# Row tiles of sixteen rows of all eight batches, in an attention-and-experts kernel on one core

## What is computed

```python
v = layernorm(x)
kv = v[:, :, :, None, :] * ctx[:, :, None, :, :]      # every pair of 8 rows in a head: (8, 32, 8, 8, 512)
y = causal_convolution(kv, k) + kv * skip             # along the 512 columns, one filter for each head
x = x + einsum('bhijl,bhil->bhjl', y, ctx)            # mix: sum over the first row index
h = layernorm(x)                                      # 2048 tokens of 512
scores = sigmoid(h @ gate_w.T); two of 8 experts for a token, weights normalized, times 2.5
x = x + shared_ffn(h) + sum over the two experts of weight * expert_ffn(h)
```

## Time and profile before

| | |
|---|---|
| time, median of 3 runs | 721.83 us (719.22 to 723.05) |
| profiled execution: its own time | 725.05 us |
| its span in the trace | 723.3 us |
| PE busy | 658.7 us, 91% |
| DVE busy | 446.4 us, 62% |
| POOL busy | 351.5 us, 49% |
| ACT busy | 309.5 us, 43% |
| TensorE clock granted, mean | 0.975 of full |
| DMA moved | 91.6 MB, 127 GB/s |

### The profile page before, as it was taken

One profiled execution on the slowest core, in us unless ns is written; L12 is line 12 of the kernel. 1 busy time (PEld: TensorE's weight loads), 2 busy tenths in 40 slices (PEclk: granted clock), 3 DMA queues, 4 the chain that ended last, 5 costly groups with the idle time before them and its releaser, 6 DMA issues.

```text
span 723.3 us, 11575 instructions
## 1 busy us (share of the span) xinstructions
PE 658.7 (91%) x3475; PEld 330.7 (46%) x3476; DVE 446.4 (62%) x689; ACT 309.5 (43%) x422; POOL 351.5 (49%) x304
## 2 busy tenths in 40 slices
PE   5989878989979989989999998798879999999993
PEld 3535334444334444443444443345445555555551
DVE  5998894899897677797887767874331221122110
ACT  5386667373306464224631295534332233323321
POOL 2999897947468524578564016200222222322232
PEclk8999988999999999999999999999999999999998
DMA  7944224321145600134214659859995788898854
GB/s 203 288 121 127 60 87 88 73 58 45 55 151 123 154 15 16 30 132 79 69 29 176 274 122 350 276 117 193 223 179 98 128 127 128 134 133 131 132 81 58
DMA packets 130520, 91.58 MB, mean 127 GB/s; under 512 B 96992, under 2 KB 110816, under 8 KB 129952
## 3 DMA queue, kind: packets, MB, share of 16 engines
q1 hardware_dynamic: 121728, 71.49, 41.0%
q0 software_dynamic: 8176, 18.75, 14.5%
q10 hardware_dynamic: 576, 0.82, 0.5%
HBM read 46.32 MB, written 25.65 MB: 100 GB/s over the span
## 4 chain that ended last, share of the span: by engine, by line
PE 46%; DVE 16%; POOL 15%; DMA 8%; ACT 7%; issue 5%; SPq 1%; POOLq 1%; DVEq 0%; ACTq 0%
PE banks L844 14%; PE banks L845 14%; PE banks L846 13%; POOL arena L665 9%; DMA out<-xf,ids 5%; POOL arena L693 4%; DVE arena L1509 2%; PE banks L936 2%; POOL arena L732 1%; ACT arena L1264 1%; DMA mixT<-x_tok 1%; PE banks L940 1%; PE banks L941 1%; DVE hm L1655 1%; DVE stats L1522 1%
## 5 line engine op out<-in xcount | busy, mean ns | idle before, releaser
L665 POOL TENSOR_TENSOR arena<-arena 128x512 f32<-128x512 f32 x120 | 140.0, 1197 | 66.6 <-DVE arena L1495 37.1
L807 POOL DMA_INDIRECT out<-xf,ids x39 | 60.5, 1552 | 194.4 <-DMA out<-xf,ids 138.2
L844 PE MATMUL banks<-arena 128*128 128x512 f16 (+1 forms) x330 | 124.9, 379 | 19.8 <-DVE arena L1509 9.4
L845 PE MATMUL banks<-arena 128*128 128x512 f16 (+1 forms) x330 | 124.8, 378 | 0.0
L846 PE MATMUL banks<-arena 128*128 128x512 f16 (+1 forms) x330 | 124.8, 378 | 0.0
L844 PE MATMUL banks<-arena,normed 128*128 x312 | 98.5, 316 | 4.3 <-issue 4.3
L845 PE MATMUL banks<-arena,normed 128*128 x312 | 98.4, 315 | 0.0
L846 PE MATMUL banks<-arena,normed 128*128 x312 | 98.4, 315 | 0.0
L1147 ACT ACTIVATE arena<-arena 128x2048 f16<-128x2048 f32 x31 | 59.1, 1905 | 91.7 <-POOL arena L665 88.9
L1873 DVE SCALAR_TENSOR_TENSOR hm<-banks,silu 128x256 f32<-128x256 f32 x39 | 16.5, 424 | 123.8 <-PE banks L846 112.8
L1509 DVE TENSOR_TENSOR arena<-banks,arena 128x512 f32<-128x512 f32 x128 | 80.3, 681 | 11.3 <-PE banks L846 11.1
(11 more groups left out here) (205 smaller groups left out, 1093.5 us busy)
## 6 DMA issues: line engine op xcount, KB each, us to landing
arena<-split_filters SPq DMA_DIRECT2D x31, 256.0 KB
arena<-in_expert_w SPq DMA_DIRECT2D x12, 544.0 KB, 7.6
stages<-in_expert_w SPq DMA_DIRECT2D x10, 544.0 KB
arena<-in_ctx_hidden SPq DMA_DIRECT2D x4, 1024.0 KB, 7.8
arena<-in_ctx SPq DMA_DIRECT2D x8, 512.0 KB, 6.5
out<-x_tok SPq DMA_DIRECT2D x6, 512.0 KB, 5.6
x_tok<-in_expert_w SPq DMA_DIRECT2D x5, 544.0 KB, 5.5
mixT<-in_expert_w SPq DMA_DIRECT2D x5, 544.0 KB
```

The source lines that it names most:

```text
L665: nc.gpsimd.tensor_tensor(kv[s % 2][:, lb * COLS:(lb + 1) * COLS].rearrange("p (b j i) -> p b j i", i=NH, j=NH), v[:, a, None, :].to_broad ...
L807: nc.gpsimd.indirect_dma_start(out=out, out_offset=bass.IndirectOffsetOnAxis(ap=ids[slot][:, 0:1], axis=0), in_=yg[slot], in_offset=None, ...
L844: nc.tensor.matmul(dst, wh, xh, start=(k == 0), stop=False)
L845: nc.tensor.matmul(dst, wh, xl, start=False, stop=False)
```

## The change

- A row tile holds sixteen rows of all eight batches (RT = 16), which are two whole heads. `x_rows`, `ctx_rows`, `out_rows`, `skip_col` and `mixT` follow; loads and stores are four DMAs of one tile in place of two of 64 partitions.
- A step needs one tile of values (`outer` waits for tile h // 2), and a tile of results is whole after two steps. mix_out and mixed_tile of tiles 0, 1 and 2 move into their own group; the order of the two turn banks is rewritten for it.
- The beginning loads tile 0 first, turns it twice (bank 4 for DVE, bank 5 for ACT) and works the first step by block of the sequence. Tiles 2 and 3 are normalized later, behind the first steps. The filter's low half goes to POOL.
- The low half of step 10 goes from POOL to DVE. row_bases (five small DVE instructions in group 1) works out the token numbers on the chip. The second half of the pair work is earlier in group 2 (whole `pairs(1)` at h = 6), and send_rows(1) and (2) end their own group.
- In the last group three tiles are normalized early, the logits stand before down(3), and the order of expert pieces is changed. In the routed loop the four id loads stand behind the first hidden tile, and the loads and splits of experts 6 and 7 are one tile earlier.

The diff, cut to its core:

```diff
-DVE_LOWS = (0, 1, 3, 5, 6, 7, 8, 9) + tuple(range(2 * HG - 2, H, 2))
+DVE_LOWS = (0, 1, 3, 5, 6, 7, 8, 9, 10) + tuple(range(2 * HG - 2, H, 2))
-    x_rows = x.rearrange("b (g r) l -> g b r l", r=RG)
+    x_rows = x.rearrange("b (g q r) l -> g q b r l", q=Q, r=RT)
+        turn_order = turns("skip", 0) + turns("prep", 1) + turns("out", 0, range(0, Q - 1))
         for g in range(1, G):
+            turn_order += turns("out", g - 1, (Q - 1,)) + turns("feed", g - 1) + [("xf", g - 1, 0)]
...
+            turn_order += turns("skip", 1) if g == 1 else []
+            turn_order += turns("prep", g + 1, range(0, 2)) + turns("out", g, (0,)) + turns("prep", g + 1, range(2, Q))
+            turn_order += [("rank", g - 1, 0)] + turns("skip", g + 1, range(0, 2)) + turns("out", g, (1, 2))
+            turn_order += turns("skip", g + 1, range(2, Q))
...
+            first_inverse_root(0)
+            filter_low()
             first_inverse_root(1)
+            outer(1)
+            outer(2)
+            first_inverse_root(2)
+            low_parts(2)
+            first_inverse_root(3)
+            outer(3)
...
+            first_prepare(0)
+            first_convolve(0)
+            first_convolve(1)
+            first_prepare(1)
+            first_convolve(2)
+            first_convolve(3)
+            convolve(1)
+            first_prepare(2)
+            first_prepare(3)
...
+            prepare(1, range(2, Q))
+            mix_out(0, 0)
+            convolve(6)
+            mix_out(0, 1)
+            convolve(7)
+            mix_out(0, 2)
             for g in range(1, G):
                 convolve(s0)
-                mix_out(g - 1, range(0, 2))
                 down(g - 2, 0)
-                mix_out(g - 1, range(2, Q))
+                mix_out(g - 1, Q - 1)
...
                 gate_up(g - 1, 3)
+                mix_out(g, 0)
                 if g < G - 1:
                     prepare(g + 1, range(2, Q))
                     ranks(g - 1)
+                    convolve(s0 + 6)
+                    skip_sum(g + 1, 0)
+                    skip_sum(g + 1, 1)
+                    gate_up(g - 1, SM - 2)
+                    mix_out(g, 1)
+                    convolve(s0 + 7)
+                    mix_out(g, 2)
+                    skip_sum(g + 1, 2)
+                    skip_sum(g + 1, 3)
+                    gate_up(g - 1, SM - 1)
...
             first_outer(3)
             first_low(2)
             first_low(3)
+            dve.wait_ge(filt_stored, 16)
+            products(0, 0, 0, range(0, 2))
+            first_moments(2)
+            low_parts(1)
+            products(0, 0, 0, range(2, LB))
+            first_moments(3)
+            total(0, 0)
+            first_shift_by(2)
+            first_shift_by(3)
             skip_product(0, 0)
             skip_product(0, 1)
+            products(1, 1, 0)
+            total(1, 1)
             skip_term(0, 0)
             skip_product(0, 2)
             skip_term(0, 1)
             skip_product(0, 3)
...
                 for h in range(4, HG):
                     low_parts(s0 + h + 1)
-                    if g == G - 1 and h == 4:
+                    if g == G - 1 and h == 4 or g == 2 and h == 6:
                         pairs(g - 1)
-                    elif g < G - 1 and h == 6:
+                    elif g == 1 and h == 6:
                         pair_ranks(g - 1)
-                    elif g < G - 1 and h == 7:
+                    elif g == 1 and h == 7:
                         pair_rows(g - 1)
+                    products(s0 + h, h, g)
+                    if g < G - 1 and h == 7 or g == G - 1 and h == 6:
+                        mixed_tile(g, 2)
+                        mixed_stats(g, 2)
+                    total(s0 + h, h)
+                    if h == 5:
+                        mixed_tile(g, 0)
...
-        pieces_behind = {1: [(6, 0), (6, 1)], 3: [(6, 2)], 4: [(6, 3)]} | {c + 5: [(7, c)] for c in range(EX_PARTS)}
+        pieces_behind = {1: [(6, 0), (6, 1)], 2: [(6, 2)], 3: [(6, 3)]} | {c + 4: [(7, c)] for c in range(EX_PARTS)}
```

536 lines of the change are left out of this document (267 added, 269 removed).

## The result

The changed kernel takes 758.25 us (median of four runs, 757.26 to 758.67) where the kernel before takes 721.97 (719.22 to 723.05): a ratio of 1.0507, 95% interval 1.0476 to 1.0538. It is 36 us slower, outside the range of the prediction. The profiled executions took 758.67 us (span 756.8) against 725.05 (723.3), 33.6 more.

The account below looks back on a forecast made before the run. PE, busy 91% of the span, was taken as the bound. Terms -1.6 + 4.9 + 5.0 - 1.9 - 2.5 - 4.1 = -0.2 gave 721.6 us on the runs' scale, leaned to 720.5; range 707 to 731.

Parts of the forecast that it names:

- The opening: From the start to the first logits: step 3 late by 5.9 us, gains behind it, sum -1.6, bounds -8 and +5.
- Its chain: Opening: POOL's queued root of tile 3 delays DVE's skip products, ACT's value moments and turn_filter(3); step 3 5.9 us late.
- The give-back: Up to the first logits: 2.8 us of mix work done earlier, 4.04 us gap shrinking by 2, slow clock of 2.7 gone.
- Group 1: Bank wait before skip_sum(2, 3) delays step 16 by 10.8 us, clock 2.5, turn gains 8.4: net +4.9, lower bound -3.
- The gain at the turn: End of group 1: fewer turned tiles, add_shared wait, slow clock and small waits gone: -8.4 us.
- Group 2: Waits before mix_out(2, 1) and skip_sum(3, 3), step 24 +7.6, clock 2, turn -4.6: net +5.0, bounds -2 and +9.
- The last group: Last group and its FFN: -1.9 us from mix under the steps, 2.5 gained from gaps of 1.17 and 3.19.
- The routed tiles: Tail: 4.34 us gap and 1.8 of clock go, hidden-tile wait grows by 2: net -4.1, bounds -8 and +1.
- The term that was too small: Routed tiles: the 3.78 us wait comes one tile earlier and grows by 2 us, behind SP's ids, stores and piece.
- The sign given for it: Trace sign in the tail: a PE gap of 2 to 5 us at the downs of routed tiles 1 or 2.
- The rivals: Four alternatives: bank waits covered 711 (0.17), opening keeps lead 714 (0.15), turn waits not repaid 728 (0.20), early pieces 725 (0.08).
- The one on the slow side: Groups 1 and 2: bank order holds PE and add_shared is late again at the turns, 728 us, chance 0.20.

Follow-up runs that it names:

- The filter experiment: Changed kernel with ACT's turn_filter(3) ahead of its value moments in the opening: 758.70 us, ratio 1.0501.
- both edits together: Changed kernel with turn_filter(3) ahead of ACT's value moments and POOL's value_root(1) behind outer(5): 756.06 us, ratio 1.0479.
- the pairs experiments: Changed kernel with pairs(0) whole at h == 6 of group 1 and send_rows(0) at that group's end: 752.97 us, ratio 1.0452.
- the bank experiment: Changed kernel with mixed_tile(g, 2) behind mixed_tile(g, 1) and mix_out(g, 2) ahead of PE's eighth step, groups 1 and 2: 756.93 us, ratio 1.0487.
- the last kernel: Changed kernel with thirteen edits combined, last added: load_filter ahead of stores and context, last stores behind the third hidden tile: 720.90 us, ratio 0.9985.
- the kernel with eleven edits: Changed kernel with six combined moves plus turn_filter(3), value_root(1), mix_out(g, 0) behind prepare, row_bases later, low_parts(s0 + 2) ahead of mixed_shift(g): 728.37 us.
- the kernel with the bank and root edits: Changed kernel with mix_out(g, 2) ahead of the eighth step and inverse_root(2) right behind send_rows(0): 757.59 us, ratio 1.0514.
- six: Changed kernel with last group's root, inverse_root(1), mix_out(0, 0), early moments, tile 2 ahead of the eighth step and id loads moved: 729.18 us, ratio 1.0103.
- ten: Changed kernel with six combined moves plus later stores, inverse_root(2) behind send_rows(0), split pairs(1), mix_out(g, 0) behind prepare, row_bases later: 739.59 us, ratio 1.0235.

## Why the prediction was wrong, step by step

**The opening: -1.6 predicted, +13.8 measured.** Its chain was right, and each member came 2 to 3 us later than said: the root of tile 3 ended at 33.47 (said 30.5), skip_product(0, 3) at 46.25 (44.1), ACT's value moments began at 46.33, turn_filter(3) at 51.76 (49.5), and PE began step 3 late by 8.2 (5.9). Three things behind it were wrong.
- *The consumer.* I stopped at turn_filter(3). The filter experiment gives nothing; behind the same value moments stands POOL with value_root(1), idle 9.38 us, and only both edits together move step 4 (5.6 late in place of 8.3; 2.2 us in the time, at the edge of the noise). The root cause of the chain, roots of tiles 2 and 3 behind outer(2), is worth 5.5 us.
- *A bank missed.* mix_out(0, 0) needs the bank that ACT is reading: 6.50 us and a slow clock of 2. I had worked out the same wait for groups 1 and 2 and did not ask it of group 0. Worth 7.5 us.
- *The give-back did not come.* I credited 7.5 us at the turn to group 1 (2.8 + 2 + 2.7). The diff puts inverse_root(1) ahead of outer(11) on POOL. It waited 7.63 us, ACT behind it 12.12, and feed_norm began at 122.28. The gap at 118.29 of 3.46 stands where the earlier trace rows had 4.04. Each queue that a moved step is put into had to be read here, and POOL's was not.

**Group 1: +4.9 predicted, +6.7 measured.** The mechanism is right: PE waits 7.82 us (said 9) before skip_sum(2, 3), released by DVE's mixed tile at 211.95, and its clock is 0.50 for the 4 us behind. The bank and the pairs experiments confirm it: they take step 16 from 19.3 late to 11.5 and to 15.4. PE starts step 16 at 220.82 in place of 194.52, which is 12.5 us more than the lateness at the first logits (said 10.8 + 2.5 = 13.3). The gain at the turn was over-sized: 5.8 us in place of 8.4. What I had as gain, the wait for add_shared, did go, but POOL's inverse_root(2) behind send_rows(0) can take its place (7.78 us on DVE in the bank experiment). The small variance instruction, L1528 in the earlier trace rows, takes 0.17 us in its new place at the turns of both groups.

**Group 2: +5.0 predicted, +2.3 measured.** Both waits are there, 2.35 (said 5.6) and 2.65 before skip_sum(3, 3). I took the whole pairs(1) as a price alone. It lets send_rows(1) start earlier, and DVE had idle time that took a part of it; that this is worth 5 us is what moving pairs(0) the same way showed.

**The last group: -4.4 predicted, +13.4 measured.** This is the largest error, and nearly all of it lies in one move of the change that I had not priced: the root of tiles 0 to 2 on POOL ahead of low_parts(31) and send_rows(2). POOL is idle 30.33 us. Low parts come at 421.58, PE waits 4.32 and runs at a clock of 0.50 for 5.6 us; the row DMAs come at 426.24 (before: 378.78), SP's piece of the expert is issued at 440.89 (before: 393.60), ACT waits 6.57 for it at 444.57, and down(2, 0) and the logits 2.87 and 3.38. I wrote that "no prepare and no skip_sum are there", and with that looked only at PE's order. Moving the root back gives 15.8 of the 18.

**The routed tiles: -4.1 predicted, -2.7 measured.** No gap stands before tile 9, as said. Expert 7's piece gives back 6.2 us there (39.7 late at tile 8, 33.5 at tile 9), where 4.34 + 1.8 were said. The term that was too small is the other one: the gap at the hidden tiles is 7.27 in place of 5.8, with SP's ids, stores and pieces ahead of the transposes. The lateness rises from 36.2 to 45.7 at tile 4 and falls to 40.0 at tile 5, where the kernel before had its gap of 3.78: 3.8 in place of 2. The sign given for it, a gap of 2 to 5 us, missed with the 7.27.

**The rivals.** None of the four had it. The one on the slow side was a wait at the turns, 3.4 us on each, 728. What the runs showed is of another kind: an instruction of one engine, put into a queue ahead of work that others need. My range was built of sizes of waits that I had found, and left nothing for a queue that I had not walked.

**What the runs leave open.** In the last kernel PE has no gap over 3.3 us behind its first 15 us, and it is level. In its profile the first logits are 0.3 us early, those of group 3 4.8 and the span 5.3, while the runs' medians agree to 0.3 us; the two don't say the same, and the interval goes by the runs. None of the thirteen edits was made to the kernel before. Several are not its old order but new ones (the filter ahead of the stores, the low parts ahead of the shift, the whole pairs(0) earlier), and what they would give there is open. So "level" compares row tiles in a mended order with the old tiles in an order that was not mended. What the pairs' early place is worth in group 2 by itself was not tried, only its split. What the thirteen edits do show: none of them changes the tiles, and with them the 36 us are gone, so the row tiles can be had without the loss. The old places restored one at a time (the last root 15.8, the root of group 1 3.7) show where much of it came from; how much of the rest is loss undone and how much is gain of a new order is not separated. A gain of the row tiles over the kernel before is not shown.

## What to carry to other kernels

Where a change moves a step, write out for every engine what stands behind it in that engine's queue and when its operand comes. A root of 1 us cost 16 us here, and the price stood in no group of busy time. When a mechanism is found in one group (a bank still being read), ask it of every other group, the first and the last ones too. And mend waits together before judging: the bank edit was worth 1.3 us alone and needed the pairs moved before its stretch came level.

## What the runs showed of the hardware

- DVE's skip products took 1.63 and 1.55 us while POOL ran its tensor products (33.43 to 42.56), and 0.74 as soon as POOL was idle. I had priced all of them at 1.5. DVE's timeline after:

```profile
34.44 1.63 DVE L1559 SCALAR_TENSOR_TENSOR hm<-arena,skip_col,normed 128x512 f32<-128x512 f32 x1
36.00 1.55 DVE L1559 SCALAR_TENSOR_TENSOR silu<-arena,skip_col,normed 128x512 f32<-128x512 f32 x1
43.51 0.74 DVE L1559 SCALAR_TENSOR_TENSOR hm<-arena,skip_col,normed 128x512 f32<-128x512 f32 x1
45.51 0.74 DVE L1559 SCALAR_TENSOR_TENSOR silu<-arena,skip_col,normed 128x512 f32<-128x512 f32 x1
```

- In proportion the wait is worst for tiny instructions: a shift of 4 elements took 3.83 us beside POOL's low parts and 0.16 elsewhere, much like the 3.41 of the earlier trace rows; a low half took 4.77 in place of 2.28. The total kept its time beside POOL's work: 2.27 mostly beside the low parts (212.03 in the kernel with eleven edits), 2.29 beside the outer products (39.98 after). Here are DVE's and POOL's timelines of the kernel with the bank and root edits, then DVE's of the one with eleven (L1528 is its low half, not the L1528 of the earlier trace rows):

```profile
228.19 3.83 DVE L1713 SCALAR_TENSOR_TENSOR shift<-meanvar,rstd 128x4 f32<-128x4 f32 x1
227.51 4.49 POOL L686 TENSOR_TENSOR arena<-arena 128x512 f16<-128x512 f32 x4
```

```profile
214.82 4.77 DVE L1528 TENSOR_TENSOR arena<-arena 128x2048 f16<-128x2048 f32 x1
```

- The Trainium skill, page SBUF — State Buffer, section SBUF: two separate sides, says that a VectorE operation in a 2-port performance mode, or with two SBUF inputs against a GpSimd operation that reads SBUF, and the GpSimd operation exclude each other for a whole instruction, and that nothing else on the engine side contends. That the one-input total keeps its 2.29 us agrees with it. By that rule the shift would wait for one of POOL's instructions, 4.49 us for four, about 1.1 (an estimate); it took 3.7 us longer, so the rule does not give the size.
- The shift ended at 232.02 and POOL's four low parts at 232.00; the 3.41 us of the earlier trace rows ended at 214.53 and POOL's four there at 214.50. In these two places DVE lost all that was left of the row of four, and at 104.74 in the kernel before, beside low parts as well, a shift took 1.04 us. What decides between the two is not shown.
- POOL's wait for its own four indirect row DMAs at the turn from group 1 to 2 was 1.82 us in the changed kernel, where SP issued the load of the context (1 MB) at 215.57, after POOL's fourth DMA instruction had ended at 214.95. It was 5.47 in the bank experiment, where that load was issued at 216.18 and the fourth ended at 216.75. It is so in every trace of this document: where the load was issued 0.6 us ahead of that end (the kernel before, six, ten and eleven edits, both kernels with the bank edit) the wait is 5.45 to 5.66 us, where it came behind, 1.8. So 3.6 us of a queued send_rows go with which of the two comes first; the load was not moved by itself.
